# Scores of two groups of four heads in one burst, in a fused cross-attention and mixture-of-experts kernel

## The reference

```python
q, k, v = heads(layernorm(x) @ Wq.T), heads(ctx @ Wk.T), heads(ctx @ Wv.T)
scores = einsum('bhqd,bhkd->bhqk', q, k) * 128 ** -0.5 + bias
x = x + (softmax(scores) @ v, heads joined) @ Wp.T
n = layernorm(x)
affinity = softmax(n @ gate_w.T)          # each expert takes the 32 best tokens of a sequence
x = x + sum over experts of gating * down(silu(gate(n)) * up(n))
```

## Time and profile before

| | us |
|---|---|
| median of 3 runs (1127.79 to 1129.33) | 1128.38 |
| profiled execution, its own time | 1129.07 |
| span of the profiled execution | 1127.3 |
| TensorE busy | 1066.8 (95%) |
| VectorE busy | 888.7 (79%) |
| ScalarE busy | 810.8 (72%) |
| GpSimd busy | 683.3 (61%) |

### The profile page before, as it was taken

How to read it: one execution, slowest core, us unless ns; L and a number is a source line. 1 busy time by engine, 2 the same in 40 slices (tenths; PEclk the granted TensorE clock), 3 DMA queues, 4 the chain that set the end, 5 groups by cost and what they waited for, 6 DMA issues and landing times. The chain is left out here.

```text
span 1127.3 us, 46562 instructions
## 1 busy us (share of the span) xinstructions
PE 1066.8 (95%) x13640; PEld 868.2 (77%) x13640; DVE 888.7 (79%) x3847; ACT 810.8 (72%) x2407; POOL 683.3 (61%) x1155
## 2 busy tenths in 40 slices
PE   4999999999999999999999999998499999999995
PEld 3888888888888888888888888886256666666664
DVE  4898898898988988989989889887765656565553
ACT  4777778777877787787778777875366666667562
POOL 5566566565665665655656656654047767767673
PEclk9999999999999999999999999999589999999998
DMA  3765555555555555555555555555001121111112
GB/s 102 121 106 109 109 100 114 105 106 111 106 103 114 100 109 107 101 114 106 105 112 105 104 113 100 111 102 86 0 11 29 29 58 37 37 56 29 50 54 66
DMA packets 307337, 96.83 MB, mean 86 GB/s; under 512 B 284256, under 2 KB 300640, under 8 KB 307296
## 3 DMA queue, kind: packets, MB, share of 16 engines
q1 hardware_dynamic: 306432, 94.16, 41.7%
q10 hardware_dynamic: 864, 2.16, 0.5%
HBM read 16.58 MB, written 4.19 MB: 18 GB/s over the span
## 5 line engine op out<-in xcount | busy, mean ns | idle before, releaser
L408 ACT ACTIVATE probs<-neg,negmax 128x120 f32<-128x120 f32 x1024 | 320.3, 383 | 157.7 <-DVE negmax L430 157.6
L430 DVE CUSTOM_DVE_ANT_0 neg<-bk_s,bias_sb 128x120 f32<-128x120 f32 x1024 | 227.5, 277 | 77.3 <-PE bk_s L550 73.7
L270 POOL CAST p_parts<-probs 128x480 f16<-128x480 f32 x256 | 150.2, 587 | 135.6 <-ACT probs L408 131.8
L1098 POOL TENSOR_TENSOR hid<-hid_f,hid 128x512 f16<-128x512 f32 x128 | 167.7, 1314 | 73.9 <-ACT hid L1052 72.9
L550 PE MATMUL bk_s<-qk 64*128 64x120 f32 x2048 | 181.4, 296 | 0.5 <-DVE negmax L430 0.5
L498 DVE TENSOR_TENSOR p_parts<-probs,p_parts 128x480 f16<-128x480 f32 x256 | 177.6, 694 | 0.7 <-POOL p_parts L270 0.5
L550 PEld LDWEIGHTS bk_s<-qk 64*128 64x128 f32 x2048 | 134.2, 186 | 45.4 <-issue 45.3
L589 PE MATMUL bk_y<-wp_sb,oT 128*128 128x128 f32 x1024 | 156.3, 275 | 0.0
L1152 DVE TENSOR_TENSOR hid_f<-bk_u,silu 128x512 f32<-128x512 f32 x128 | 88.3, 690 | 85.3 <-ACT silu L1045 35.0
L378 ACT COPY qk<-bk_a 128x496 f32<-128x496 f32 x256 | 144.7, 565 | 3.3 <-PE bk_a L537 3.3
L589 PEld LDWEIGHTS bk_y<-wp_sb,oT 128*128 128x128 f32 x1024 | 134.5, 191 | 0.2 <-ACT oT L371 0.2
(11 more groups left out here) (161 smaller groups left out, 3399.9 us busy)
## 6 DMA issues: line engine op xcount, KB each, us to landing
y_all<-y SPq DMA_DIRECT2D x128, 64.0 KB, 2.0
wst<-ffn_w SPq DMA_DIRECT2D x64, 96.0 KB, 2.3
x_sb<-x SPq DMA_DIRECT2D x64, 64.0 KB, 2.0
pT<-p_parts SPq DMA_TRANSPOSE x256, 3.1
out<-x_sb SPq DMA_DIRECT2D x16, 256.0 KB, 2.0
ctx_f<-ctx_t SPq DMA_DIRECT2D x64, 60.0 KB, 1.9
w_f<-wqkv_t ACTq DMA_DIRECT2D x3, 512.0 KB, 5.4
wp_sb<-wp_t ACTq DMA_DIRECT2D x1, 512.0 KB, 6.2
```

What stands on the lines that cost most here:

```text
L270: pool.tensor_copy(p_parts[g][:, 0, :, 0:K], probs[g % 2][:, :, :]).then_inc(p_hi_ready, 1)
L408: e = nc.scalar.activation(probs[g % 2][:, i, :], neg[g % 2][:, i, :], ACT.Exp, bias=negmax[g % 2][:, i:i + 1], scale=-1.0)
L430: r = nc.vector.tensor_tensor_reduce(out=neg[g % 2][:, i, :], in0=bk_s[i % 2][:, (i // 2) * K:(i // 2 + 1) * K], in1=bias_sb[:, :], scale= ...
L1098: nc.gpsimd.tensor_tensor(hid[1][par][:, ic, :], hid_f[ic % 2][:, :], hid[0][par][:, ic, :], ALU.subtract).then_inc(hid_lo_ready, 1)
```

## The change

TensorE computes scores in every second step only (g = 0 and 2), then for two groups, g and g + 1, one after the other; the second group's scores go to columns 240 to 479 of the same two banks. VectorE reads the columns of its group. In even steps it waits for the scores of both groups before it reads the first (while TensorE still writes the second group, the banks are not to be read); in odd steps they are already there. TensorE waits for q and k of both groups and for VectorE to be through with the group before.

```diff
@@ VectorE
-                    dve.wait_ge(scores_written, n + 1)
+                    dve.wait_ge(scores_written, n + 2 - g % 2)
...
-                            out=neg[g % 2][:, i, :], in0=bk_s[i % 2][:, (i // 2) * K:(i // 2 + 1) * K],
+                            out=neg[g % 2][:, i, :], in0=bk_s[i % 2][:, (g % 2 * GP + i // 2) * K:(g % 2 * GP + i // 2 + 1) * K],
@@ TensorE
-                if live(t - 1):
+                if live(t - 1) and g % 2 == 0:
 
                     p1 = (par + 1) % 2
-                    pe.wait_ge(qk_ready, n + 1)
+                    pe.wait_ge(qk_ready, n + 2)
                     if some(n):
                         pe.wait_ge(neg_ready, n)
-                    for j in range(GP):
-                        for h in range(2):
-                            r = slice(DH * h, DH * (h + 1))
-                            m = nc.tensor.matmul(bk_s[h][:, j * K:(j + 1) * K], qk[p1][r, g, j * S:(j + 1) * S],
-                                                 qk[p1][r, g, GP * S + j * K:GP * S + (j + 1) * K],
-                                                 start=True, stop=True)
-                    m.then_inc(scores_written, 1)
+                    for gs in (g, g + 1):
+                        for j in range(GP):
+                            at = (gs - g) * GP + j
+                            for h in range(2):
+                                r = slice(DH * h, DH * (h + 1))
+                                m = nc.tensor.matmul(bk_s[h][:, at * K:(at + 1) * K], qk[p1][r, gs, j * S:(j + 1) * S],
+                                                     qk[p1][r, gs, GP * S + j * K:GP * S + (j + 1) * K],
+                                                     start=True, stop=True)
+                        m.then_inc(scores_written, 1)
```

## The result

The changed kernel takes 1145.03 us (median of 4 runs, 1144.52 to 1145.21) against 1128.24 for the kernel before, a ratio of 1.0143 (95% interval 1.013 to 1.0155). The time lies 0.03 us outside the range.

What follows compares the result with a forecast made beforehand. A ring of VectorE, GpSimd and TensorE was taken to bound the slot: 6.25 + 4.38 + 1.41 = 12.04 against 11.96 us, +4.8 us over 60 slots; with 1.8 for the port, +6.6, so 1135.0 us; range 1121 to 1145.

Steps and rivals of the forecast that it cites:

- What bounds the kernel: Attention slot: waits among VectorE, GpSimd and TensorE set its 11.96 us, rather than TensorE's throughput.
- The ring: VectorE, GpSimd and TensorE waiting on each other in turn, 6.25 + 1.27 + 3.48 + 0.96 = 11.96 us a slot.
- What the change takes away and adds: TensorE's bursts: 0.58 us less work a slot; VectorE's step 0 waits 0.45 us longer, step 2 hides its wait.
- What is late next: TensorE's step 3 without its burst: `x2T` is the last input, 4.38 us from step 2's `neg` to the burst, 4.75 before.
- a sign of being wrong: Trace checks that would refute the forecast: 6.25 us arc changed over 0.1, gate finding `x2T` ready, slot below 11.9 us.
- The port: Shared by VectorE and GpSimd: an earlier `xn` could delay GpSimd's cast; 0.03 us a slot taken, 1.8 us in all.
- The lower bound: For `xn` and GpSimd's cast at the shared port: cast not moved, 0 us; the upper bound was 0.25 us.
- Restarts: TensorE in step 3: 0.05 us from `x2T` to the weight load, and 0.08 us for restarting from standstill.
- Rivals: Four alternatives: port delaying cast, 1148 us (0.13); port helping, 1119 (0.13); no change, 1127 to 1130 (0.17); TensorE throughput, 1093 (0.05).
- rival 4: TensorE's throughput decides, so entering and leaving 120 bursts is saved: -35 us, 1093 us; chance 0.05.
- rival 1: At the shared port `xn` delays GpSimd's cast by 0.25 us: +0.33 a slot, some +20 us, 1148 us; chance 0.13.
- the first arc: VectorE's `neg` of step 0 to `neg` of step 2, through GpSimd's chain: 6.25 us, kept but for 0.03.

## Why the prediction was wrong

- *What bounds the kernel*: right. The ring gave the slot before, and moving GpSimd's cast or either pair moved the time by about what the measured arcs say.
- *What the change takes away and adds*: right. The wait of step 0 was priced at 1.41 us from burst to `neg` and measured 1.40; step 2 hid its wait; steps 1 and 3 lost theirs.
- *What is late next*: this step failed. I listed `o_sb`, the copy of q and k and `x2T` as the inputs of TensorE's step 3 and let `x2T` end last, 4.38 us from `neg` to burst. It is 4.56. `x2T` came when I had said, 3.61 us after `neg`, but the gate found it ready, which I had named as a sign of being wrong. `oT` is not in my list. The buffer it empties, `bk_x`, is the output of the transposes, which come before the projection that reads `oT`, so the wait is for a free buffer and not for data. With 0.18 us a slot it makes 11 us, about the 10.2 that I was short. The move of that one copy returned 15 us and put the arc at 4.27, the figure for `o_sb`. It also brought `x2T` forward, to 3.34 us after `neg`; so no run shows the 4.38 that I had for `x2T` alone.
- *The port*: 0.03 us a slot was allowed, and none came in the changed kernel; the arc stayed at 6.25. The lower bound was right.
- *Restarts*: I took 0.05 us from a producer's end to the waiting weight load; here it is 0.13 after `o_sb` (415.44 to 415.57) and 0.11 after `oT`.
- *Rivals*: none of the four happened. TensorE's throughput, rival 4, decides only where GpSimd's cast is moved as well, in the kernels at 1110.4 and 1091.7 us. The upper end of the range was there for rival 1; that the time came within 0.03 us of it is luck.
- *The remainder*: 0.25 us in each of 60 slots is 15 us of the 16.8. In the two profiled executions the last group of scores is read 15.4 us later (791.54 rather than 776.12 us from the start) and the span is 15.9 us longer (1143.2 rather than 1127.3). What is left between that and 16.8 is less than the 1.5 us by which the runs of the kernel before differ.

## What to carry to other kernels

When work is taken out of one engine of a ring, list for each instruction that moves up every wait it has, those for free buffers as well as those for data, and time them all from the event that stays fixed; the gain ends at the latest of them. Merging two bursts into one saves one entering and leaving (0.29 us here), but makes the first consumer wait for the second half: that is free only where the consumer is late by itself, here in one step of four. So try the halves of a symmetrical change apart: one was worth -13 us, the other +28.

## What the runs showed of the hardware

`xn` on VectorE, 0.33 us long in other kernels, was recorded at 0.72 in the changed kernel, from 411.96 to 412.68. GpSimd's next cast is recorded 0.06 us later than `xn`, kept its 0.58 and was over 0.08 us before `xn`. I read this as `xn` having waited for it.

```profile
411.25 0.71 POOL L300 TENSOR_SCALAR wsc<-wst 128x192 f32<-128x192 f32 x1
412.02 0.58 POOL L270 CAST p_parts<-probs 128x480 f16<-128x480 f32 x1
```

In the changed kernel with `oT` moved, `xn` was recorded at 406.10, 0.05 us before `wsc` was over, and kept its 0.33; there the cast was stretched:

```profile
405.44 0.71 POOL L300 TENSOR_SCALAR wsc<-wst 128x192 f32<-128x192 f32 x1
406.22 0.65 POOL L270 CAST p_parts<-probs 128x480 f16<-128x480 f32 x1
```

It is the same in all ten slots from 300 to 420 us of both kernels (`xn` 0.72 to 0.74, the cast 0.58; `xn` 0.33, the cast 0.65). So rival 1 exists, at 0.06 us a slot rather than 0.25 (6.31 rather than 6.25 for the first arc), and a shift of some 0.06 us in `xn` goes with the change of who waits. The order of the recorded starts doesn't tell the winner. The waiting shows up as a longer instruction and not as idle time, so it is found by comparing an instruction's duration with itself elsewhere.
